# A transformer block on one core: rows of the first layer norm turned by DMA and VectorE instead of TensorE

## What is computed

```python
def _layernorm(x, axis=-1, eps=1e-05):
    m = jnp.mean(x, axis=axis, keepdims=True)
    v = jnp.var(x, axis=axis, keepdims=True)
    return (x - m) / jnp.sqrt(v + eps)

    Q = x @ Wq.T + bq
    K = x @ Wk.T + bk
    V = x @ Wv.T + bv
    scores = jnp.einsum('bqd,bkd->bqk', Q, K) / jnp.sqrt(jnp.asarray(d, x.dtype))
    scores = scores * _gaussian_mask(x.shape[1], x.dtype)
    attn = jax.nn.softmax(scores, axis=-1)
    out = jnp.einsum('bqk,bkd->bqd', attn, V)
    return out @ Wo.T + bo

    bw1 = _binarize(w1)
    h = jnp.einsum('bsd,hd->bsh', x, bw1) + b1
    h = jax.nn.gelu(h, approximate=False)
    bw2 = _binarize(w2)
    out = jnp.einsum('bsh,dh->bsd', h, bw2) + b2

    x = x + _L0_attn_ref(_layernorm(x, axis=-1), ...)
    x = x + _L0_ffn_ref(_layernorm(x, axis=-1), ...)
```

## Time and profile before

| | |
|---|---|
| time, median of 3 runs | 1491.53 us (1489.79 to 1492.05) |
| span of the profiled execution, first to last instruction | 1486.6 us |
| PE busy | 1460.9 us, 98% |
| DVE busy | 1030.6 us, 69% |
| POOL busy | 835.7 us, 56% |
| ACT busy | 787.6 us, 53% |
| 16 DMA engines, queue q1 | 25.0% |

### The profile page before, as it was taken

How to read it: one execution, slowest core, us unless ns; L and a number is a source line. 1 busy time by engine, 2 the same in 40 slices (tenths; PEclk the granted TensorE clock), 3 DMA queues, 4 the chain that set the end, 5 groups by cost and what they waited for, 6 DMA issues and landing times.

```text
span 1486.6 us, 24033 instructions
## 1 busy us (share of the span) xinstructions
PE 1460.9 (98%) x9421; PEld 1327.1 (89%) x9421; DVE 1030.6 (69%) x1681; ACT 787.6 (53%) x951; POOL 835.7 (56%) x1097
## 2 busy tenths in 40 slices
PE   8999999999999999999999999999999999999997
PEld 6889989999898998989999898998989999899986
DVE  7567776767767667776776767677675777767574
ACT  5564654646556464654646556465564646546341
POOL 3564637556374673637656375673646746375553
PEclk9999999999999999999999999999999999999999
DMA  5312412223121332403214122231303224121220
GB/s 191 81 34 43 128 27 75 71 57 114 36 76 60 71 100 43 123 19 73 86 48 124 29 71 72 65 106 44 100 29 82 89 44 128 25 75 44 57 86 29
DMA packets 86060, 106.16 MB, mean 71 GB/s; under 512 B 9390, under 2 KB 77372, under 8 KB 85948
## 3 DMA queue, kind: packets, MB, share of 16 engines
q1 hardware_dynamic: 85920, 104.63, 25.0%
q10 hardware_dynamic: 28, 0.01, 0.0%
HBM read 20.72 MB, written 16.78 MB: 25 GB/s over the span
## 4 chain that ended last, share of the span: by engine, by line
PE 91%; DMA 2%; DVE 2%; ACT 2%; SPq 1%; issue 1%; POOL 1%; POOLq 0%
PE ps L889 22%; PE ps L1075 15%; PE ps L927 8%; PE ps L928 8%; PE ps L907 7%; PE ps L909 7%; PE ps L908 7%; PE ps L873 2%; PE ps L874 2%; PE ps L875 2%; PE ps L935 2%; PE ps L856 2%; PE ps L857 2%; PE ps L859 2%; PE ps L840 2%; DMA prob<-prob 2%
## 5 line engine op out<-in xcount | busy, mean ns | idle before, releaser
L322 POOL TENSOR_TENSOR ptl<-pt,pth 128x512 fp32r<-128x512 f32 x256 | 327.1, 1299 | 188.3 <-ACT pth L460 188.3
L907 PE MATMUL ps<-vh,pth 128*128 128x258 f32 x1024 | 293.6, 287 | 2.9 <-POOL ptl L322 2.9
L340 POOL TENSOR_TENSOR xin<-xin,ys 128x256 f32<-128x256 f32 x128 | 94.6, 740 | 353.4 <-DVE ys L668 353.3
L909 PE MATMUL ps<-vh,ptl 128*128 128x258 f32 x1024 | 288.9, 282 | 0.0
L908 PE MATMUL ps<-vl,pth 128*128 128x256 f32 x1024 | 288.4, 282 | 0.0
L460 ACT ACTIVATE pth<-pt 128x1024 fp32r<-128x1024 f32 x128 | 135.8, 1061 | 251.2 <-DVE pt L615 251.1
L927 PE MATMUL ps<-sgn,gh 128*128 128x256 f32 x1024 | 248.6, 284 | 6.1 <-DVE gl L650 6.1
L928 PE MATMUL ps<-sgn,gl 128*128 128x256 f32 x1024 | 248.5, 284 | 0.0
L609 DVE TENSOR_REDUCE nmax<-ps 128x1 f32<-128x1024 f32 x128 | 156.5, 1223 | 120.1 <-PE ps L889 120.1
L447 ACT ACTIVATE prob<-ps,nmax 128x1024 f32<-128x1024 f32 x128 | 142.8, 1115 | 181.6 <-DVE nmax L609 181.4
L615 DVE STREAM_TRANSPOSE pt<-prob 128x1024 f32<-128x1024 f32 x128 | 158.8, 1241 | 67.4 <-DMA prob<-prob 67.2
(11 more groups left out here) (116 smaller groups left out, 2798.0 us busy)
## 6 DMA issues: line engine op xcount, KB each, us to landing
prob<-prob SPq DMA_DIRECT2D x512, 128.0 KB, 3.1
xin<-in_L_attn_x_dram SPq DMA_DIRECT2D x32, 512.0 KB, 4.5
out_dram<-xin SPq DMA_DIRECT2D x31, 512.0 KB, 3.8
w1s<-in_L_ffn_w_dram SPq DMA_DIRECT2D x1, 1024.0 KB, 10.0
w2s<-in_L_ffn_w_dram SPq DMA_DIRECT2D x1, 1024.0 KB, 12.0
mask_bc<-mask_dram SPq DMA_DIRECT2D x1, 512.0 KB, 7.1
out_dram<-xin SPq DMA_DIRECT2D x1, 384.0 KB, 2.4
wk<-in_L_attn_Wk_dram SPq DMA_DIRECT2D x1, 256.0 KB, 4.8
```

What stands on the lines that cost most here:

```text
L322: pool.tensor_tensor(ptl[:, q % P_SLOTS, half(n)], pt[:, q % P_SLOTS, half(n)], pth[:, q % P_SLOTS, half(n)].bitcast(F32), ALU.subtract).t ...
L907: pe.matmul(with_sum, pth[:, q % P_SLOTS, tile(j)], vh[:, j, 0:D + 2], start=j == 0, stop=False)
L909: last = pe.matmul(with_sum, ptl[:, q % P_SLOTS, tile(j)], vh[:, j, 0:D + 2], start=False, stop=j == T - 1)
```

## The change

The normalised rows of the first layer norm no longer pass through PE. ACT writes `xn1` in blocks of 32 columns. SP regroups a half with four DMAs of 128 KB from SBUF to SBUF (`regroup_rows`), of the same shape as those of the probabilities, into `first_rows` for batch 0 and `later_rows` for the others. DVE transposes 32x32 blocks (`turn_rows`, one instruction of 128x1024 for a half) into `kmf` in SBUF. `hi_rows`, `lo_rows` and `mask_keys` then read `kmf` instead of PSUM, and `mask_keys` overwrites it in place, so that it waits for `lo_rows` (`xl_set`).

Since rows come out in another order of partitions, x is loaded twice: as `xrow` for statistics and normalising, and as `xin` (two slots instead of three, loaded one batch ahead) in the new order for what is added. The store and the mask follow the new order.

In the lists: DVE turns half 0 after `turn_probs(4)` and half 1 after `turn_probs(5)`, and does `lo_rows` of half 0 ahead of `turn_probs(6)`. ACT does `hi_rows` of half 0 ahead of `hi_probs(5)`, and that of half 1 right after the exponentials of q = 7. SP issues `regroup_rows` of half 0 ahead of `regroup_probs(4)` and of half 1 ahead of `regroup_probs(5)`, and the `xrow` loads of batch b + 2 behind `regroup_probs(7)`. In the start, `regroup_rows` of batch 0 stands behind the loads of the weights, and DVE turns both halves ahead of the first `lo_rows`.

```diff
-X_SLOTS = 3
+X_SLOTS = 2
...
-    out_v = out.rearrange("b (p t) d -> b p t d", t=T)
+    x_res = x.rearrange("b (e u t) d -> b u e t d", u=16, t=T)
+    out_v = out.rearrange("b (e u t) d -> b u e t d", u=16, t=T)
...
+            def regroup_rows(b, n):
+                sp.wait_ge(xn1_set, T * b + TH * (n + 1))
+                if b >= 2 and n == 0:
+                    sp.wait_ge(ffn_scaled, T * (b - 1))
+                for i in range(P // QUAD):
+                    sp.dma_start(regrouped_rows(b, n)[i * QUAD:(i + 1) * QUAD, :],
+                                 xn1[:, n, i, :]).then_inc(rows_back[n], 16)
+
+            def load_rows(b, n):
+                sp.wait_ge(xn1_set, T * b)
+                sp.dma_start(xrow[:, n * TH:(n + 1) * TH, :],
+                             x_v[b, :, n * TH:(n + 1) * TH, :]).then_inc(rows_in[n], 16)
...
                 for q in range(TH, T):
+                    if more and q < TH + N2:
+                        regroup_rows(b + 1, q - TH)
                     regroup_probs(b, q)
+                if b + 2 < B:
+                    for n in range(N2):
+                        load_rows(b + 2, n)
                 if b > 0:
                     for n in range(N2):
                         store(b - 1, n, slice(n * TH, (n + 1) * TH), T)
-                    if b + 2 < B:
+                    if more:
                         for n in range(N2):
-                            load(b + 2, n)
+                            load(b + 1, n)
...
-                act.activation(xh[:, :, half(n)], slot(n), ACT.Copy).then_inc(xh_set, 1)
+                act.activation(xh[:, :, half(n)], kmf[:, n], ACT.Copy).then_inc(xh_set, 1)
...
+            def turn_rows(b, n):
+
+                dve.wait_ge(rows_back[n], 64 * (b + 1))
+                dve.transpose(kmf[:, n].rearrange("p c s -> p (c s)").rearrange("p (j g r) -> p g j r", g=P // QUAD, r=QUAD),
+                              regrouped_rows(b, n).rearrange("p (g j s) -> p g j s", g=P // QUAD, s=QUAD)).then_inc(x_turned, 1)
 
             def lo_rows(b, n):
                 dve.wait_ge(xh_set, N2 * b + n + 1)
-                dve.tensor_tensor(xl[:, :, half(n)], slot(n), xh[:, :, half(n)].bitcast(F32),
+                dve.tensor_tensor(xl[:, :, half(n)], kmf[:, n], xh[:, :, half(n)].bitcast(F32),
                                   ALU.subtract).then_inc(xl_set, 1)
 
             def mask_keys(b, n):
 
                 m = mask_bc[:, half(n)].unsqueeze(1).broadcast_to([P, C, HALF])
-                dve.scalar_tensor_tensor(out=kmf[:, :, half(n)], in0=slot(n), scalar=1.0, in1=m,
+                dve.wait_ge(xl_set, N2 * b + n + 1)
+                dve.scalar_tensor_tensor(out=kmf[:, n], in0=kmf[:, n], scalar=1.0, in1=m,
                                          op0=ALU.add, op1=ALU.mult).then_inc(km_set, 1)
...
+                if more:
+                    hi_rows(b + 1, 0)
                 hi_probs(b, 5)
...
+                    if more and q in (1, 2):
+                        turn_rows(b + 1, q - 1)
                 if not more:
                     last_tail(b, s)
                     return
+                lo_rows(b + 1, 0)
                 turn_probs(b, 6)
-                lo_rows(b + 1, 0)
                 add_attention(b, s, 4)
                 mask_keys(b + 1, 0)
...
-            def turn_rows(b, n, first=False):
-
-                pe.wait_ge(xn1_set, T * b + TH * (n + 1))
-                if not first:
-                    pe.wait_ge(exp_set, T * (b - 1) + T - 1 + n)
-                for t in range(TH):
-                    for c in range(C):
-                        last = pe.transpose(ps[:, 2 * n + c, tile(t)].rearrange("p (r g) -> p g r", r=QUAD),
-                                            xn1[:, TH * n + t, tile(c)],
-                                            ident[:].rearrange("p (g r) -> p g r", r=QUAD))
-                last.then_inc(x_turned, 1)
...
-                turn_rows(b + 1, 0)
                 weigh_values(b, 4)
-                turn_rows(b + 1, 1)
                 weigh_values(b, 5)
```

More of the change, by code:

```diff
@@ L157, in preln_attention_ffn @@
         x_loaded = [[sem(f"x_loaded{s}_{n}") for n in range(N2)] for s in range(X_SLOTS)]
+        rows_in = [sem(f"rows_in{n}") for n in range(N2)]
+        rows_back = [sem(f"rows_back{n}") for n in range(N2)]
         y_stored = [sem(f"y_stored{n}") for n in range(N2)]
@@ L236, in _ @@
             sp.dma_start(w2s[:], w2.rearrange("(c p) h -> p c h", p=P)).then_inc(w2_loaded, 16)
-            for s in range(1, X_SLOTS):
-                for n in range(N2):
-                    sp.dma_start(xin[s][:, n * TH:(n + 1) * TH, :],
-                                 x_v[s, :, n * TH:(n + 1) * TH, :]).then_inc(x_loaded[s][n], 16)
+            def regroup_rows(b, n):
[7 more added lines that the diff above has]
+                sp.wait_ge(xn1_set, T * b)
+                sp.dma_start(xrow[:, n * TH:(n + 1) * TH, :],
+                             x_v[b, :, n * TH:(n + 1) * TH, :]).then_inc(rows_in[n], 16)
             def regroup_probs(b, q):
@@ L273, in batch @@
                         regroup_probs(b + 1, q)
+            for n in range(N2):
+                regroup_rows(0, n)
+            for n in range(N2):
+                load_rows(1, n)
+            for b in range(X_SLOTS):
+                for n in range(N2):
+                    load(b, n)
             for q in range(TH):
@@ L513, in batch @@
                 if more:
-                    normalize_attention(b + 1, (b + 1) % X_SLOTS, range(TH))
+                    normalize_attention(b + 1, range(TH))
                 exponentials(b, 4)
@@ L517, in batch @@
                 if more:
-                    normalize_attention(b + 1, (b + 1) % X_SLOTS, range(TH, T))
+                    normalize_attention(b + 1, range(TH, T))
                     normalize_ffn(b, s, 0)
@@ L671, in head @@
             def head(b, rows_of):
-                r, loads = (b + 1) % X_SLOTS, (b + 1) // X_SLOTS + 1
                 def next_stats(tiles):
                     if b + 1 < B:
-                        dve.wait_ge(x_loaded[r][tiles.start // TH], 16 * loads)
-                        stats_attention(r, tiles)
+                        dve.wait_ge(rows_in[tiles.start // TH], 16 * (b + 2))
+                        stats_attention(tiles)
                 def rows_scaled(rows):
@@ L758, in _ @@
                                      op1=ALU.subtract).then_inc(ml_set, 1)
+            for n in range(N2):
+                turn_rows(0, n)
             for n in range(N2):
@@ L991, in _ @@
             pe.wait_ge(bvb_set, C)
-            for n in range(N2):
-                turn_rows(0, n, True)
             for m in range(C):
@@ L1011, in _ @@
             pe.wait_ge(diag_set, C)
-            pe.wait_ge(km_set, N2)
             for c in range(C):
```

59 lines of the change are left out of this document (33 added, 26 removed).

## The result

The changed kernel takes 1522.56 us (median of four runs, 1521.17 to 1523.19), beside 1491.66 for the kernel before: the ratio is 1.0211, with a 95% interval of 1.0197 to 1.0226. It is 30.9 us slower. The forecast was 1515, 23.5 slower, with a range of 1496 to 1558.

The account below looks back on a forecast made before the run. The prediction took PE, busy 98% of the span, as the bound until something it waits for comes too late. Span 1486.6 + 15 (turns) + 8.5 (start) = 1510, plus 4.9 from span to median: 1515 us, range 1496 to 1558.

Parts of the forecast that it names:

- the turn that it worked through: Batch 6 ending and 7 beginning: PE saves 1.75 us, waits 2.75, mostly for `ql`; net +1.0.
- The tie at `mask_keys(0)`: `mask_keys(0)` and GpSimd's `lo_probs` of q=6 start 0.02 us apart every batch and exclude each other; VectorE taken as first.
- The signs: Expected in the profile after: `ql` bracket of 1.5 us or more, four SP issues before q=5, `row_max` of q=7 1.5 late.
- The one on `mask_keys`: Sign: `mask_keys` and `lo_rows` means above 1.3 us; prediction wrong if `mask_keys` stays at 1.2 beside GpSimd.
- the turn's term: Net cost in the steady turns: +1.0 us a turn, 15 us in fifteen.
- fourteen others look like it: Assumption that the other turns match the one from batch 6 to 7, so its +1.0 us was applied to fifteen.
- The start: Before the first scores: eight row transfers between normalising and splitting, behind the weights, cost +8.5 us, ends 4.5 and 10.5.
- The last term: Added to the span of 1510: 4.9 us by which the median of the runs exceeds the profiled span.
- The price of the collision: VectorE instructions with two SBUF inputs and GpSimd ones exclude each other: turn +1.0 us with this, +0.25 without.
- GpSimd goes first: Rival, tie the other way: PE waits 3.85 us in one piece, clock at 0.50, +3.7 a turn, 1555; chance 0.22.
- No collision: Rival: the tie slips apart or a lone GpSimd half is hidden; +0.25 us a turn, 1504; chance 0.17.
- Faster, as PE's list says: Rival: half 1's transfers don't delay q=5, `row_max` of q=7 stays; gains 1.2 us a turn, 1482; chance 0.14.

Follow-up runs that it names:

- e3: Changed kernel with the regrouping of rows half 1 behind that of q=5 on SyncE and its VectorE transposes behind `row_max` of q=7: 1511.6 us, ratio 1.0139.
- e2: Changed kernel with `lo_rows` and `mask_keys` reading their first input from PSUM in all batches but the first: 1521.9 us, ratio 1.0215.
- e11: Changed kernel with the edits of e2 and e3 together: 1492.7 us, ratio 1.0012.
- e1: Kernel before, with one PE transpose instead of eight for a half of the rows in each turn, nothing in their place: 1478.3 us, ratio 0.9924.
- e8: Changed kernel with the order of e3, and VectorE, ScalarE and GpSimd lists reordered (both `lo_rows` before turn q=6, first two `lo_queries` before `mask_keys`): 1485.9 us, ratio 0.9966.
- e13: Changed kernel with e8's lists, batch 0's rows transposed by PE, and ScalarE's last two `hi_queries` ahead of `normalize_ffn` of tile 5: 1466.6 us, ratio 0.9843.
- e12: Changed kernel with e8's lists, batch 0's rows transposed by PE, and `add_attention` of q=7 ahead of `mask_keys` of half 1 on VectorE: 1482.2 us, ratio 0.9947.
- e10: Changed kernel with a VectorE transpose of 384 columns ahead of `mask_keys(0)` in each turn: 1568.6 us, ratio 1.0524.
- e6: Changed kernel with a VectorE memset of 64 columns ahead of `mask_keys(0)` in each turn: 1520.6 us, ratio 1.0209.
- e7: Changed kernel with a VectorE memset of 384 columns ahead of `mask_keys(0)` in each turn: 1528.1 us, ratio 1.0251.
- e4: Changed kernel with the loads of w1 and w2 issued behind the regrouping of batch 0's rows: 1517.9 us, ratio 1.0183.

## Why the prediction was right, and where its sizes were off

**The chain.** In the turn that it worked through, the prediction held to one or two tenths of a microsecond. Offsets, predicted and measured: landing of q=5 20.5 and 20.4; `row_max` of q=7 24.1 and 24.0; `turn_probs(7)` 32.2 and 32.2; `mask_keys(1)` 34.6 and 34.6; `ql` 35.7 and 35.8; the third group of queries 36.5 and 36.7. The tie at `mask_keys(0)`, VectorE first, came as written, the clock stayed up, and PE's pieces, forecast at 0.3, 0.8 and 1.65, were 0.3, 0.7 and 1.7 from start to start. It gave +1.0 for this turn; 90.99 - 89.81 is +1.2.

**The signs.** The `ql` bracket (1.52 in every steady turn), SP's four issues, the late q=5 and the late `row_max` came. The one on `mask_keys` was badly put. It asked for a mean above 1.3 and called the prediction wrong if `mask_keys` stays at 1.2 beside GpSimd. It did stay, at 1.19, as the prediction's own order of events had it, with VectorE first; what grew was `lo_rows`, to a mean of 1.82, and GpSimd's pair.

**The step that failed in the turn's term** is "fourteen others look like it". They averaged +1.45. In the changed kernel the length of a turn is the offset of q=5's landing plus 70.55, within 0.2, in each of the fourteen, and this landing came at 20.1 to 21.3; the chosen turn lies low among them. In the turn from 1163.41, the latest, the fourth transfer of q=3 kept SP for longer (four issues in 3.73 us, 2.58 in the chosen turn), and behind it came, one after the other, ScalarE's `hi_probs(3)`, the last four normalised tiles, the rows of half 1 and q=5. Fifteen turns at +1.0 were 15; the records show 22.0, and of the 7 between them the worked turn's own 0.2 explains some 3 and the spread some 4. e3 shows the reason: with the rows behind q=5 all turns last 90.6.

**The start** was forecast at 8.5 late, with ends 4.5 and 10.5; it was 11.7. The failing step is the upper end. It let eight transfers follow w2 at their own pace, and left w2's landing at 17.7. The two ran at the same time: w2 landed at 20.69, the last rows at 25.46, and the rows took 7.5 us in the median instead of 3.4. `lo_rows` began at 26.65, 1.35 past the latest time given. In the eight profiled kernels with this start the loss is 9.2 to 12.6, so 8.5 was too low in each.

**The sum.** 15 + 8.5 = 23.5 were forecast. The records have 22.0 + 11.7 + 1.1 (tail) = 34.8, so the span was forecast 11.3 short. The last term hid a third of this by luck: the prediction added 4.9 us for what lies between span and median, and in the changed kernel that is 1.2. Only 1.8 lie outside a span; the rest was that a fast execution of the kernel before had been profiled. So the 1515 was 7.6 short, all of it in sizes.

**The price of the collision** was put at 0.75 a turn (1.0 against 0.25). In the changed kernel's own order it is near that: without it `ql` of the worked turn comes 0.83 earlier (offset 34.97 in e2, 35.80 with it), 0.96 in the mean of the fourteen, and e2's short turns are +0.3 over before, for +0.25. The 1.23 from e11 to e3 belongs to another order. In e2 VectorE still waits 0.46 for the landing of q=7, as the prediction had it, and this hides a part; in e11 it doesn't wait there, and nothing is hidden.

**The rivals.** "GpSimd goes first" was real. The prediction named 0.02 us as its margin; by the records a lead of 0.10 is enough (e1), and one of 0.01 the other way leaves VectorE first. Its price was 3.7 and measured 4.5, the pause of 0.5 included. "No collision" at 1504 was wrong in its consequence: e2 had none and took 1521.9, since a wait in one piece, of 1.9 to 2.5 us, was followed by a clock of 0.50 in nine turns. The prediction had counted only waits above 2.8 as dangerous, from one row of 2.83. "Faster, as PE's list says" was wrong in its condition: q=5 did land late. The nearest test is e3, which brought `row_max` back to 22.63 and still took 1511.6, since the transposes then stood in the chain behind it: `ql` at offset 35.4, against the 34.3 of this rival (630.25).

## What to carry to other kernels

Work taken from the bounding engine is worth only as much as the next wait on it allows: about half of it here, even at no cost elsewhere (e1). Before moving work, find what that wait hangs on, and reorder the lists so that its chain runs first. The change as it stood lost 2.1%. With its chain to `ql` put first it won 0.3% (e8), and with batch 0 back on PE and ScalarE's list mended as well, 1.6% (e13). An item moved for one engine can stand in the list of another (e12): look at every engine that waits for what was moved back. When one turn is costed for many, look at how far its landings spread over the others before multiplying.

## What the runs showed of the hardware

- Whether PE's clock falls to the lower level depends on more than the length of the wait before. One piece of 1.91 us was followed by 0.50, one of 2.28 was not (e2); 1.52 behind one or two smaller pieces never was (changed kernel, fourteen turns); 3.65 always was (e10).
- A GpSimd instruction of 128x1 is held up by a VectorE instruction with two SBUF inputs just as a large one is: 1.07 us for 0.19 (e12).
- A VectorE instruction with two SBUF inputs that starts 0.10 us behind GpSimd's subtraction is held up by it (2.27 us for 1.2; e1, and 0.11 behind in e6 and e8). A VectorE memset of 384 columns that starts 0.10 behind is not: it keeps GpSimd off, and so does the two-input instruction right after it, 0.40 behind (e7). A transpose in the memset's place doesn't (e10).
- Eight transfers of 128 KB issued behind 2 MB of loads took 7.5 us each in the median, and 3.4 ahead of them (e4).
